# Delta stage: the lower left 16x16 block of a group's triangular inverses by small TensorE products

## The reference, cut to what matters

```python
def step(S, xs):
    qc, kc, vc, bc = xs
    kb = kc * bc[:, None]
    A = jnp.tril(kb @ kc.T, -1)
    U = solve_triangular(eye + A, vc * bc[:, None] - kb @ S, lower=True)
    o = qc @ S + jnp.tril(qc @ kc.T) @ U
    return (S + kc.T @ U, o)
```

## Time and profile before

| What | Before |
|---|---|
| Median of 3 runs | 1425.33 us (1423.44 to 1427.81) |
| Span of the profiled execution | 1419.9 us |
| PE busy | 996.3 us (70%) |
| PEld busy | 734.6 us (52%) |
| DVE busy | 1131.7 us (80%) |
| ACT busy | 685.8 us (48%) |
| POOL busy | 789.5 us (56%) |
| Mean granted clock of TensorE | 0.796 |

### The profile page before, as it was taken

One profiled execution on the slowest core, in us unless ns is written; L12 is line 12 of the kernel. 1 busy time (PEld: TensorE's weight loads), 2 busy tenths in 40 slices (PEclk: granted clock), 3 DMA queues, 4 the chain that ended last, 5 costly groups with the idle time before them and its releaser, 6 DMA issues.

```text
span 1419.9 us, 32994 instructions
## 1 busy us (share of the span) xinstructions
PE 996.3 (70%) x11963; PEld 734.6 (52%) x11963; DVE 1131.7 (80%) x3199; ACT 685.8 (48%) x1510; POOL 789.5 (56%) x668
## 2 busy tenths in 40 slices
PE   4537768678785556399999955655455599999960
PEld 1214455545554445278888842323223378888850
DVE  1188899998999874389888846999999889788845
ACT  2444354452533212177777734444444277777740
POOL 3232256666565452527777651167777647777660
PEclk9778779586785655599999986777766599999985
DMA  5010101111111114149788832011211549788839
GB/s 134 23 45 25 47 24 59 37 50 46 55 58 37 49 32 164 37 138 307 253 292 281 282 117 92 30 63 63 68 38 34 194 160 296 252 282 287 280 110 350
DMA packets 78625, 184.34 MB, mean 130 GB/s; under 512 B 16735, under 2 KB 44826, under 8 KB 68224
## 3 DMA queue, kind: packets, MB, share of 16 engines
q1 hardware_dynamic: 51280, 142.04, 29.7%
q0 software_dynamic: 17280, 35.70, 7.2%
q10 hardware_dynamic: 9904, 4.49, 1.2%
HBM read 131.20 MB, written 52.79 MB: 130 GB/s over the span
## 4 chain that ended last, share of the span: by engine, by line
DVE 34%; PE 32%; POOL 12%; issue 10%; ACT 5%; DMA 4%; SPq 1%; POOLq 0%; DVEq 0%; ACTq 0%
PE ps L1539 5%; POOL res L668 4%; DVE seq L1172 4%; POOL xs L630 4%; PE ps L1747 2%; PE ps L1748 2%; PE ps L1749 2%; POOL rn L613 2%; PE ps L1761 2%; PE ps L1759 2%; PE ps L1760 2%; DVE prod L787 2%; DVE t_p L791 2%; DVE r_stats L709 2%; DMA res<-orow,idt 2%
## 5 line engine op out<-in xcount | busy, mean ns | idle before, releaser
L630 POOL DMA_INDIRECT xs<-ysc,slot_u x256 | 281.4, 1099 | 186.7 <-DVE slot_u L930 114.7
L668 POOL DMA_INDIRECT res<-orow,idt x284 | 292.3, 1029 | 144.7 <-issue 79.2
L1094 DVE TENSOR_TENSOR hidl<-hidf,hidh 128x512 fp32r<-128x512 f32 (+1 forms) x320 | 199.2, 637 | 21.1 <-ACT hidh L1408 15.1
L1406 ACT ACTIVATE hidf<-ps,wb 128x512 f32<-128x512 f32 (+1 forms) x320 | 198.3, 654 | 4.2 <-PE ps L1749 3.7
L1747 PE MATMUL ps<-yTh,wb 128*128 128x512 f32 (+1 forms) x320 | 126.3, 395 | 0.0
L1759 PE MATMUL ps<-hidh,wb 128*128 128x512 f32 (+1 forms) x320 | 124.5, 389 | 0.0
L1749 PE MATMUL ps<-yTh,wb 128*128 128x512 f32 (+1 forms) x320 | 119.2, 372 | 0.0
L1748 PE MATMUL ps<-yTl,wb 128*128 128x512 f32 (+1 forms) x320 | 119.1, 372 | 0.0
L1761 PE MATMUL ps<-hidh,wb 128*128 128x512 f32 (+1 forms) x320 | 117.8, 368 | 0.0
L1760 PE MATMUL ps<-hidl,wb 128*128 128x512 f32 (+1 forms) x320 | 117.4, 367 | 0.0
L1416 ACT ACTIVATE out_t<-ps,wb 128x512 f32<-128x512 f32 (+1 forms) x80 | 51.3, 642 | 111.9 <-PE ps L1761 111.9
(11 more groups left out here) (259 smaller groups left out, 2573.4 us busy)
## 6 DMA issues: line engine op xcount, KB each, us to landing
wb<-wblob SPq DMA_DIRECT2D x80, 1032.0 KB, 5.6
xt<-xs SPq DMA_DIRECT2D x62, 288.0 KB
wblob<-hl SPq DMA_DIRECT2D x16, 512.0 KB
fin<-res SPq DMA_DIRECT2D x14, 512.0 KB, 10.3
hidf<-res SPq DMA_DIRECT2D x10, 512.0 KB, 4.1
res<-orow,idt POOLq DMA_INDIRECT x284
xs<-ysc,slot_u POOLq DMA_INDIRECT x256
rs<-res SPq DMA_DIRECT2D x8, 512.0 KB, 4.7
```

The costliest lines, as they stand in the source:

```text
L630: pool.indirect_dma_start(xs[:, :], bass.IndirectOffsetOnAxis(slot_u[:, g % 2, k, n:n + 1], 0), ysc[:, g % 2, n, :], None).then_inc(s(f"mo ...
L668: pool.indirect_dma_start(res[m][:, :], bass.IndirectOffsetOnAxis(idt[:, t % IR, j:j + 1], 0), orow[:, t % OR, j, :], None, bounds_check=2 ...
L1094: ve.tensor_tensor(hidl[:, t % 2, c, 0:n], hidf[:, t % 2, c, 0:n], hidh[:, t % 2, c, 0:n].bitcast(F32), ALU.subtract)\
L1406: ins = act.activation(hidf[:, t % 2, c, 0:n], ps[:, c, 0:n], ACT.Gelu_apprx_tanh, bias=b_col)
```

## The change

The row-by-row part stays on DVE, but its 15 rows are spread over slots 1 to 22 (`B_ROWS`: 1, 2, 4, 5, 7, 8, 10, 11, 13, 14, 16, 17, 19, 20, 22). The eight pieces go. Right after row 15 and `place`, in slot 23, DVE transposes the inverses with an empty lower left block into t_c (semaphore `d_tc`) and the upper 16 rows of the diagonal inverses once more, as d_n (`d_dn`). In slot 24 the PE multiplies each of the 128 matrices' n_c with the right half of t_c (128 products of 32x32 by 16 columns, into bank BK_B), in slot 25 ACT copies the result to SBUF (`below`), in slot 27 the PE multiplies 16x16 tiles of d_n and `below` (128 products), and in slot 31 DVE adds the result from PSUM to the right half of t_c, scaled per partition by head_of (`d_inv`, for which UW waits). d_n and `below` lie in the buffer of the squares (sq), so ACT's squares of a group wait for the second round of the group two before it (`d_corner`).

```diff
-        B_INV = 1
-        B_SECOND = (16, 18, 22, 25, 26, 28, 29, 32)
-        B_TC = 34
+        B_ROWS = tuple(i + i // 2 + 1 for i in range(SUB - 1))
+        B_TC = 23
+        B_BELOW = 24
+        B_CORNER = 27
+        B_ADD = 31
...
-                i = t - B_INV + 1
+                i = B_ROWS.index(t) + 1 if t in B_ROWS else 0
...
-                k = B_SECOND.index(t) if t in B_SECOND else -1
-                if 0 <= k < 4 and step == 0:
-                    m0, n = 4 * k, SUB - 4 * k
-                    ch.wait(marks["row"])
-                    marks["prod"] = ch.mark(ve.tensor_tensor(
-                        prod2[:, 0:4 * SUB * n].rearrange("p (m l j) -> p m l j", m=4, l=SUB),
-                        bc(n_p[:, SUB:C, m0:SUB], 1, 4), bc(t_p[:, m0:m0 + 4, m0:SUB], 2, SUB), ALU.mult))
...
             def stage_b(g, t):
                 if t == B_TC:
...
                     ve.transpose(t_c[:, :, :, :].rearrange("p n h i -> p i (n h)"),
-                                 t_p[:, :, :].rearrange("p m l -> p l m")).then_inc(s("d_inv"), 1)
+                                 t_p[:, :, :].rearrange("p m l -> p l m")).then_inc(s("d_tc"), 1)
+                    ve.transpose(d_n.rearrange("p k m -> p m k"), t_p[:, 0:SUB, :]).then_inc(s("d_dn"), 1)
+                if t == B_ADD:
+                    right = t_c[:, :, :, SUB:C].rearrange("p n h i -> p (n h) i")
+                    ve.wait_ge(s("d_tc"), g + 1)
+                    ve.wait_ge(s("d_corner"), g + 1)
+                    ve.scalar_tensor_tensor(right, ps[:, BK_B, :].rearrange("p (k i) -> p k i", i=SUB), head_of[:, 0, 0:1], right,
+                                            ALU.mult, ALU.add).then_inc(s("d_inv"), 1)
...
+                    if g >= 2:
+                        act.wait_ge(s("d_corner"), g - 1)
                     act.activation(sq[:, hb], kqv[:, hb, 0:KQ], ACT.Square).then_inc(s("d_sq"), 1)
...
+            def stage_b(g, t):
+                if t == B_BELOW + 1:
+                    act.wait_ge(s("d_below"), g + 1)
+                    act.copy(below, ps[:, BK_B, :].rearrange("p (k i) -> p k i", i=SUB)).then_inc(s("d_belows"), 1)
...
+            def stage_b(g, t):
+                if t == B_BELOW:
+                    pe.wait_ge(s("d_tc"), g + 1)
+                    pe.wait_ge(s("d_uw"), g * CG)
+                    pe.wait_ge(s("d_kqv"), min(g + 2, B) * BPB)
+                    for k in range(BPB * HEADS):
+                        n, h = divmod(k, HEADS)
+                        for q in range(Q):
+                            ins = pe.matmul(ps[rows_of(q), BK_B, k * SUB:(k + 1) * SUB], n_c[rows_of(q), n, h, :],
+                                            t_c[rows_of(q), n, h, SUB:C], start=True, stop=True, skip_group_check=True)
+                    ins.then_inc(s("d_below"), 1)
+                if t == B_CORNER:
+                    pe.wait_ge(s("d_dn"), g + 1)
+                    pe.wait_ge(s("d_belows"), g + 1)
+                    for k in range(BPB * HEADS):
+                        for q in range(Q):
+                            top = slice(C * q, C * q + SUB)
+                            ins = pe.matmul(ps[top, BK_B, k * SUB:(k + 1) * SUB], d_n[top, k, :], below[top, k, :],
+                                            start=True, stop=True, skip_group_check=True)
+                    ins.then_inc(s("d_corner"), 1)
```

More of the change, by code:

```diff
@@ L220, in hybrid_kernel @@
         prod = prod_all[:, :].rearrange("p (b m l) -> p b m l", b=2, m=SUB)
-        corner = prod_all[:, 0:SUB * SUB].rearrange("p (m l) -> p m l", m=SUB)
-        prod2 = n_c[:, :, :, :].rearrange("p n h j -> p (n h j)")
+        solved = sq[:, :, :].rearrange("p n k -> p (n k)")
+        d_n = solved[:, 0:BPB * HEADS * SUB].rearrange("p (k m) -> p k m", m=SUB)
+        below = solved[:, BPB * HEADS * SUB:2 * BPB * HEADS * SUB].rearrange("p (k i) -> p k i", i=SUB)
         vp = sb1("vp", [2, 2, HEADS * DV])
@@ L1372, in _ @@
                     if 0 <= i + 1 < B:
+                        stage_b(i + 1, t)
                         apply(i + 1, 0, t)
```

## The result

The changed kernel takes 1526.7 us (median of 4 runs, 1523.63 to 1531.53), the kernel before beside it 1426.23 (4 runs, 1423.44 to 1427.81): a ratio of 1.0715 (95% interval 1.0688 to 1.0742), 100 us slower. The forecast was 63 us slower, 1488 us, with a range to 1508. The side is right, the size is not. (A run's time is here 1.8 us above the span of its profile, 1528.14 and 1526.3, and not some 5 us as stated ahead of the prediction; the forecast keeps the same difference on both sides, so its growth of 63 us doesn't hang on that.)

The account below looks back on a forecast made before the run. DVE was the bound on average, but PE's fixed order would decide behind slot_u; 11 us (first two groups), 38 (four middle) and 14 (last two) gave +63, 1488 us; own range 1465 to 1505, 8 in 10 1435 to 1508.

Parts of the forecast that it names:

- DVE's saving: Per group, eight pieces removed, d_n and an add put in: net 13.1 us less DVE work, buying nothing behind slot_u.
- P to slot_u, +0.7: Middle group, from POOL's second power of ro to slot_u's end: 0.7 us longer, bounds 2.5 sooner to 1.5 later.
- t_c's wait: Behind slot_u, PE waits in order for DVE's transpose t_c, which ends 2.0 us after slot_u.
- The rounds, 5.2 and 4.2 us: Two added PE rounds of 256 records each per group, priced by similar products' running time: together 9.4 us.
- the forecast's signs of being wrong: Rounds of 3 us or less, clock 1.00 from slot_u on, or POOL's ro power following its last send at once everywhere.
- UW's wait, -1.0: Behind the convolution in a middle group, UW no longer waits for t_c: 1.0 us off.
- Sum: All eight inverses: +5.5 us each for the first two, +9.5 for four middle ones, +7 for the last two; +63.
- kn: First group: kn comes at 97.15 us in place of 99.75, as the sums before POOL's power come 2.6 us sooner.
- Rival (a): Rounds run at clock 1.00, 3.2 us each, and the convolution's time halves: +29 us, 1454 us; chance 0.23.
- Rival (b): Both rounds take 6.0 us with pauses between records, +2.6 us per group: 84 us more, 1509 us; chance 0.06.
- (c): Short rounds fit PE's idle time, convolution no later than slot_u + 6.8 us, POOL the limit: -13, 1412 us; chance 0.12.
- (d): Gains and losses cancel, with rounds of 2.4 us: 1425 us; chance 0.04.

Follow-up runs that it names:

- new order: Four-products kernel with DVE rows 13 to 15 before the choice of experts, t_c at slot 18, d_n at slot 25: 1410.97 us, ratio 0.9916.
- four products a round: Changed kernel with only 4 products in each round, other inverses not the right ones: 1442.7 us, ratio 1.0144 to the kernel before.
- the doses: Changed kernel (1526.7 us) with half of the added instructions, 1464.1 us, and with a quarter, 1437.0 us; as many columns in each.
- the quarter run: Changed kernel with 32 products of 64 columns a round in place of 128 of 16, inverses not right: 1437.0 us, ratio 1.0074.

## Why the prediction came out too small

- **DVE's saving.** Forecast 13.1 us a group, and that it buys nothing: both right (101 us less busy, no gain). It buys nothing in this order of DVE; in the new order, with four products a round, the kernel is 14 us under the one before.
- **P to slot_u, +0.7.** n_p to slot_u is 36.4 to 36.5 us in the middle groups in place of 36.0 to 36.2, so 0.2 to 0.4. Within the bounds given.
- **t_c's wait.** Forecast slot_u + 2.0; PE starts round one at 308.12, slot_u + 1.9. Right.
- **The rounds, 5.2 and 4.2 us: the step that failed.** The records themselves are faster than forecast: 249 in 3.86 us and 256 in 2.7 (0.40 + 1.25 + 1.02). So one of the forecast's signs of being wrong, rounds of 3 us or less, holds for round two's records; with its pauses the round lasts 6.0 us (316.42 to 322.45). What the sum did not have is the pause for instructions, 1.71 + 0.88 + 2.48 + 2.17 = 7.2 us up to the convolution. The forecast priced a round by the running time of its records and took their supply as given, at no cost. The duration of a record came from rows of 64 and 128 records, which don't show what a longer run meets. By the end of the qn transposes the two errors cancel (forecast slot_u + 10.1, measured 316.49 - 306.24 = 10.3); behind round two they no longer do: the convolution starts at slot_u + 19.6, forecast 15.5.
- **UW's wait, -1.0.** The wait is gone (338.26 follows without a gap), but the stretch from convolution to n_p is 19.0 us as before (19.1): n_c waits for the gram products as it did, and a pause for instructions of 0.81 us (at 342.96, behind 56 of UW's 64 records) stands where one of 0.56 us stood before (at 354.47, behind 54). A wait that was not the last to end is worth nothing when removed.
- **Sum.** Middle groups grew by 15.5, 14.9, 11.8 and 14.1 us, forecast 9.5; the first two by 9.4 and 10.3, forecast 5.5; the seventh by 13.2, forecast 7. In a middle group the convolution is 4.1 us later than forecast and UW's 1.0 us doesn't come: 9.5 becomes some 14. In the eighth the transposes of o come at slot_u + 25.5 (the answer to the earlier trace rows), forecast 20.5:

```profile
623.34 1.09 PE L1667 MATMUL ps<-ident,o 128*128 128x128 f32 x4 [3.41 <-issue]
```

- **In the first group** kn comes at 95.86 us, 3.9 us sooner than before; forecast 97.15. The group is longer all the same, by the pauses: the rounds, from 100.37 to 114.33, hold 1.52, 2.41 and 2.47 us of them.

Rival (a), clock 1.00, did not come: the granted clock was 0.50 from 306 to 331 us and 0.99 behind. Rival (b) named pauses between records, but priced them with 2.6 us a group, where the pauses up to the convolution measure 7.2; its 1509 us falls short by 18, and the range ended at 1508. Rivals (c) and (d) needed short rounds. A run gave them: with a quarter of the instructions, in the change's own order, a middle group's rounds take 1.9 and 1.3 us and the convolution starts 8.4 to 9.9 us behind slot_u, as (c) reckoned (9.2); yet the kernel takes 1437.0 us, where (c) had 1412 and (d) 1425. What both left out is the cost of DVE's order, which the run with four products a round shows. With that order mended the convolution starts 5.6 to 6.8 us behind slot_u, inside (c)'s condition, and the kernel takes 1404.65, but (c) did not have that order; how much of the nearness to its 1412 is luck, no run tells.

As for the rule of about 60 cycles per matmul (the Trainium skill, "TensorEngine Tiling (Array Packing)", section Instruction Overhead): that 4 columns cost what 16 do agrees (round one: 190 against 210 ns a record, 8.3 against 8.2 us busy in two groups; the kernels take 1525.51 and 1526.7 us); the 6.4 us a round estimated from it does not, at 4.0 and 2.7 us of running time and a clock of 0.50. The pauses are not in that rule.

What is shown is that the loss goes by the number of added instructions beyond the first 256 a group, not by columns, and that other work between them gives part of it back. That the cause is the arrival of the 16 KB packets is read from the traces (the equal spacing, 128 records between pauses, one packet in each window, each start 1.4 to 1.5 us behind a packet's end); the fetch itself was not changed by a run. The doses agree with it: summed over the stage, PE's pauses of over 0.2 us with no releaser that end 1.1 to 1.7 us behind a packet are 9 us in the kernel before, 11 with a quarter of the rounds, 27 with a half and 66 in the changed kernel.

The granted clock fell as well: the middle groups have a mean of 0.68 to 0.70, before 0.74 to 0.77. No run parts this from the pauses, but it is small here: PE is busy 53.0 us in a group in place of 45.5, and the rounds alone are 6.7 of the 7.6 us more, so an estimated 1 us a group is left for it. Between the quarter run and the changed kernel it is some 2 of the 11 us a group: the convolution takes 3.7 to 4.5 us there and 4.8 to 6.4 here.

## What to carry to other kernels

Moving work to an idle engine as many tiny instructions has a price that no busy time shows: count the instructions (the queue "q8 instruction" counts them in packets), and where a run of products is shorter in time than the packets that bring it, price it by packets: 3.7 us per 256 here. Work taken from the busiest engine pays only if what is left is put where that engine waits: here three rows and two transposes on the wrong side of one wait cost some 26 to 32 us, more than the 14 us that the kernel then gained over the one before. Fewer and wider instructions (two matrices per product, masked, in one pass) plus the better order turned 100 us of loss into 9 of gain.

## What was not expected of the hardware

- PE's instructions came at 3.7 us per packet of 256 (three intervals of 3.68 to 3.76 us; 3.4 and 3.9 us from the doses), while a packet of 16x16 products runs in 1.25 us at a clock of 0.50. About one packet per group is free (1437.0 against 1442.7 us with 4 products a round, 1404.65 against 1410.97 in the new order).
- A small product at 0.50 takes less time on a smaller tile: 128 records of 16x16 tiles in 1.25 us (9.8 ns each), 249 of 32x32 tiles in 3.86 (15.5 ns). Its columns hardly count: with 4 in place of 16, round one is busy 8.3 against 8.2 us in two groups.
- More products can help: in the new order the run with a quarter of the rounds is 6 us faster than that with 4 products a round (ratios to before 0.9853 and 0.9916, their intervals apart), at a mean clock of 0.809 against 0.794. That the clock is the cause was not tried.
